# Moving the gate-logit fills of a transformer layer behind a group of products with the values

## The reference

```
x = x + 0.5 * ffn(layernorm(x))
x = x + attention(layernorm(x))      # 16 heads of 16, causal, softmax, output projection
x = x + 0.5 * ffn(layernorm(x))
```

```
probs = softmax(x @ gate_w.T)                    # 8 experts: the gate logits
top2_w, top2_idx = top_k(probs, 2)
counts = bincount(top2_idx); keep = counts <= cap   # cap = 1.25 * 8192 / 8
out = sum over the two experts of  keep * weight * expert(x)
```

## Time and profile before

| what | value |
|---|---|
| median of 3 runs | 1375.12 us |
| the profiled execution, its own time | 1374.71 us |
| its span | 1373.0 us |
| PE busy | 1273.9 us (93%) |
| DVE busy | 1093.9 us (80%) |
| ACT busy | 942.2 us (69%) |
| POOL busy | 397.3 us (29%) |
| chain that ended last | PE 61%, DVE 21%, ACT 6%, issue 3%, DVE's queue 3%, DMA 2% |

### The profile page before, as it was taken

How to read it: one execution, slowest core, us unless ns; L and a number is a source line. 1 busy time by engine, 2 the same in 40 slices (tenths; PEclk the granted TensorE clock), 3 DMA queues, 4 the chain that set the end, 5 groups by cost and what they waited for, 6 DMA issues and landing times.

```text
span 1373.0 us, 25088 instructions
## 1 busy us (share of the span) xinstructions
PE 1273.9 (93%) x8693; PEld 600.0 (44%) x8693; DVE 1093.9 (80%) x3527; ACT 942.2 (69%) x1697; POOL 397.3 (29%) x508
## 2 busy tenths in 40 slices
PE   6899999999999999999999999999999999999884
PEld 4433334444454444454444444544445544444332
DVE  6888888778887888878887788878888788779634
ACT  2257777777767777767767777677777677676752
POOL 3223322333232322332323332323222323222111
PEclk9889999999999999999999999999999999999977
DMA  4580443543325443324435423254442243340001
GB/s 134 114 156 13 70 70 58 100 75 74 68 37 100 90 70 70 61 63 89 70 59 101 83 62 68 40 101 89 70 70 53 38 92 70 58 69 32 1 1 34
DMA packets 57832, 95.18 MB, mean 69 GB/s; under 512 B 8352, under 2 KB 51488, under 8 KB 51744
## 3 DMA queue, kind: packets, MB, share of 16 engines
q1 hardware_dynamic: 55664, 92.30, 35.7%
q10 hardware_dynamic: 2032, 1.19, 0.3%
HBM read 59.91 MB, written 33.55 MB: 68 GB/s over the span
## 4 chain that ended last, share of the span: by engine, by line
PE 61%; DVE 21%; ACT 6%; issue 3%; DVEq 3%; DMA 2%; POOL 1%; SPq 1%; ACTq 0%; POOLq 0%
PE o_bank L1319 15%; PE s L1300 14%; PE st L1285 12%; DVE s L1011 8%; PE misc L1202 6%; PE misc L1186 4%; PE misc L1194 4%; DVE max_full L1015 3%; ACT probs L860 3%; PE misc L543 3%; DVE xn L519 2%; ACT q_stack L847 2%; DVEq L1022 2%; DVE stats L510 1%; DVE o_tok L1108 1%
## 5 line engine op out<-in xcount | busy, mean ns | idle before, releaser
L860 ACT ACTIVATE probs<-st 128x512 f32<-128x512 f32 (+1 forms) x1216 | 632.5, 581 | 192.2 <-PE st L1285 119.0
L1011 DVE CUSTOM_DVE_ANT_0 s<-s,causal 128x128 f32<-128x128 f32 (+3 forms) x1024 | 493.4, 502 | 131.9 <-PE s L1300 127.2
L1300 PE MATMUL s<-k_stack,q_stack 96*128 96x512 bf16 (+3 forms) x1536 | 493.7, 332 | 33.1 <-DVE max_full L1015 13.4
L1285 PE MATMUL st<-q_stack,k_stack 108*128 108x512 bf16 (+3 forms) x1536 | 486.8, 331 | 11.7 <-ACT probs L860 11.2
L1015 DVE TENSOR_REDUCE max_full<-s 128x1 f32<-128x512 f32 x512 | 349.7, 683 | 46.6 <-PE s L1300 46.3
L1319 PE MATMUL o_bank<-probs,v_aug 128*17 128x512 f32 (+3 forms) x3072 | 326.0, 496 | 5.4 <-POOL probs L734 5.2
L1300 PEld LDWEIGHTS s<-k_stack,q_stack 96*128 96x128 bf16 x1536 | 149.7, 98 | 373.1 <-DVE max_diag L1011 167.1
L734 POOL TENSOR_SCALAR_AFFINE_SELECT probs<-probs 128x512 f32<-128x512 f32 x256 | 163.5, 639 | 473.2 <-ACT probs L860 472.7
L1285 PEld LDWEIGHTS st<-q_stack,k_stack 108*128 108x128 bf16 x1536 | 149.8, 98 | 108.3 <-ACT probs L860 39.2
L746 POOL TENSOR_TENSOR qk<-qk,parts 128x512 f32<-128x512 f32 x64 | 75.0, 1171 | 282.4 <-ACT parts L820 282.4
L847 ACT ACTIVATE q_stack<-misc 12x2048 bf16<-12x2048 f32 x63 | 117.8, 1870 | 41.3 <-PE misc L1267 40.9
(11 more groups left out here) (115 smaller groups left out, 879.2 us busy)
## 6 DMA issues: line engine op xcount, KB each, us to landing
part_dram<-parts SPq DMA_DIRECT2D x128, 192.0 KB, 2.8
k_stack<-part_dram SPq DMA_DIRECT2D x186, 128.0 KB, 6.9
q_stack<-part_dram SPq DMA_DIRECT2D x31, 384.0 KB, 5.1
x_all<-x SPq DMA_DIRECT2D x16, 512.0 KB, 11.5
q_stack<-part_dram SPq DMA_DIRECT2D x31, 256.0 KB, 7.4
out<-x_all SPq DMA_DIRECT2D x7, 1024.0 KB, 10.6
q_stack<-part_dram SPq DMA_DIRECT2D x33, 128.0 KB, 9.0
k_stack<-part_dram SPq DMA_DIRECT2D x12, 64.0 KB, 3.0
```

Source lines behind the costliest of these rows:

```text
L860: nc.scalar.activation(probs[:, g % 2, h - part:h + 1, 0:width], st_bank[i % 3][:, 0:share * width] .rearrange("p (h c) -> p h c", c=width ...
L1011: nc.vector.tensor_tensor_reduce(out=bank, in0=bank, in1=causal[:, CW - width:CW], scale=1.0, scalar=-BIG, op0=ALU.add, op1=ALU.max, accum ...
L1285: score = nc.tensor.matmul(st_bank[i % 3][:, part * width:(part + 1) * width], k_stack[0:KROWS + MROWS, hg, h, jb * P:(jb + 1) * P], q_sta ...
L1300: nc.tensor.matmul(s_bank[u % 3][:, 0:width], q_stack[0:KROWS, hm, h, ib * P:(ib + 1) * P], k_stack[0:KROWS, hm, h, j0:j0 + width], start= ...
```

## The change

Two things change in the plan. First, in units that are multiples of four (those with a `pv`), `lg` and `lg0` events go from `extra` to `mid`, and so stand directly behind `pv` and ahead of `s`. Second, the units in `PLACE` are set to such multiples: `lg` 33 to 32 in step 2 and 31 to 32 in step 3; `lg0` stays at 12 in step 2 and goes from 11 to 12 in step 3.

```diff
-    "gate0": (4, 19, 23, 33, 36),
+    "gate0": (4, 19, 23, 32, 36),
...
-    "gate1": (4, 17, 26, 31, 37),
+    "gate1": (4, 17, 26, 32, 37),
...
-    "before": ((12, 16), (11, 29)),
+    "before": ((12, 16), (12, 29)),
...
     mid = {}
     for u, events in list(extra.items()):
+        if u % HG == 0:
+            mid[u] = [e for e in events if e[:2] in (("use", "lg"), ("use", "lg0"))]
+            events = extra[u] = [e for e in events if e not in mid[u]]
         for e in events:
             if e[0] == "use" and e[1] in PIECES:
```

## The result

The changed kernel takes 1372.01 us (median of 20 runs, 1370.48 to 1374.51), the kernel before 1374.3 us beside it (20 runs, 1372.34 to 1377.46): 0.9984 times, with a 95% interval of 0.9978 to 0.999. The forecast was a fall of 2.35 us, to 1372.8 us from the median then shown (1375.12). The size of the fall was met; two of its terms, for places B and C, were not, and they nearly cancel.

The account below looks back on a forecast made before the run. The bound changes hands within a batch: VectorE at A and C, TensorE at D, both close at B. 1.38 + 0.30 + 0.57 + 0.10 = 2.35 us off, 1372.8 us from the median 1375.12; range 1370.8 to 1376.2 us.

Parts of the forecast that it names:

- B: `lg` of step 2: VectorE takes the bound from TensorE, gain 0.05 us x 6 = 0.30 us in batches 1 to 6.
- C: `lg0` of step 3, 499.9 to 518.4 us: VectorE busy all along, gain 0, bounded by 0 and 0.45 x 6.
- D: `lg` of step 3, 518.4 to 532.0 us: TensorE-bound, shared column-tile visit saves 0.23 us x 6 = 1.38 us.
- A: `lg0` of step 2, 464.8 to 481.2 us: fill still waits for `o_tok`, score 0.78 us later, VectorE loses nothing; gain 0.
- from `st` 34 on TensorE is 0.23 us earlier: Step at B: behind the shared visit TensorE runs 0.23 us earlier, until it meets VectorE's shifted operations at the maximum of 496.68.
- 496.07 + 0.43 + 0.1 = 496.60: Step at B: VectorE's preceding operation, delayed 0.43 us, lets the maximum of 496.68 start at 496.60, leaving at most 0.08 us.
- Batch 0: First batch, no normalising on VectorE: 0.34 us at A and 0.23 us at C, together 0.57 us, between 0 and 0.8.
- Batch 7: Last batch: 0 at B; at D `ont` starts at 1334.0 instead of 1334.07; gain 0.10 us, between -0.3 and 0.58.
- Rival 1: Fill and `pv` do not share the column-tile visit; D gives 0, B costs 0.6 us: 1375.7 us, chance 0.18.
- Rival 2: At B VectorE packs small operations closer, so TensorE's 0.23 us come through: 1.1 us more, 1371.7 us; chance 0.22.
- rival 3: Maxima starve behind the fill at A, with B's delay uncovered too: 1380.4 us, 1377.9 with half of A; chance 0.07.
- Rival 4: Time saved at D ends in a wait before the next batch's VectorE stretch: 1374.2 us; chance 0.07.

Follow-up runs that it names:

- pair with the earlier unit: Kernel before and changed kernel, each with step 3's normalisation begun at unit 3 instead of 4: 1370.19 us (0.9979) and 1368.53 us (0.9971).
- C alone: Against the kernel before, only `lg0` of step 3 moved directly behind `pv`, the other three fills as before: 1373.77 us, 1.0009.
- D alone: Against the kernel before, only `lg` of step 3 moved directly behind `pv`, the other three fills as before: 1371.18 us, 0.9991.
- A, C and D: Changed kernel with `lg` of step 2 put back in unit 33 behind `s`, the other three fills moved: 1371.54 us, 0.9988 of the kernel before.

## Why the prediction came out right, term by term

**D** (forecast 1.38 us): right in mechanism and size. The visit is shared, the spacing is 1.95 us, and the chain keeps it: 0.24 us in D's interval of each of six batches, 1.44 us. With the fill behind the score the interval is as before.

**A** (0): right. The fill starts where it did, the score is 0.79 us later (forecast 0.78), VectorE is without idle time, and the interval stays at 14.21 us.

**B** (a gain of 0.30): wrong in sign. It is a loss of 0.05 us a batch, 0.3 us in all. The step that failed is "from `st` 34 on TensorE is 0.23 us earlier". It is not: the later maximum frees its score bank later, and the score that takes this bank waits for it (496.04), so the 0.23 us are gone before the place where I let both engines meet. I had followed the delay down VectorE's queue, but not back over the banks to TensorE. "496.07 + 0.43 + 0.1 = 496.60" failed besides: `max_rest` came at 497.38 - 0.91 = 496.47, 0.40 us later as foreseen, but lasts 0.20 us longer beside the selection, and the next maximum begins 0.29 us behind its start instead of 0.1. No run separates the two, but the times do in part. The score of 497.35 would let the maximum begin at about 497.61, by the 0.26 us between the two before (496.42 to 496.68): 0.02 us later than it was. VectorE takes it at 497.67, without idle time behind the long `max_rest`. So the wait for the bank alone takes the whole gain away, and so would the longer `max_rest` alone; the last 0.06 us are those of `max_rest`. The ends that I gave, -0.07 to +0.23, held the result.

**C** (0): right for TensorE, wrong as a sum. "The pattern of batch 2 repeats to 0.03 us at nearly all places" passed over this one, and the step "what is late next is VectorE, busy all along" treated VectorE's busy time as fixed, and it was not: an instruction in it is 0.40 or 0.88 us long, by where GpSimd's selection falls. In the traced kernel before, four batches of six were long: 4 x -0.28 + 2 x 0.21 = -0.7 us. The pair with the earlier unit, where this is taken away, gives 0.02 us a batch in C's interval (14.33 and 14.31).

**Batch 0** (0.57): 0.40. A gave its 0.34 us (13.62 to 13.26 in its interval). C gave 0.05 instead of 0.23: the `pv` ahead of the fill waits 0.19 us for GpSimd (195.51, `<-POOL probs`), and joining saves little behind a wait.

**Batch 7** (0.10): at D the step is confirmed and small, and at B one was missed. At D, from the start of `x_all` to `ont` it was 1334.07 - 1331.44 = 2.63 us, and is 1332.12 - 1329.64 = 2.48 now; before, and then after:

```profile
1331.44 0.69 DVE L1119 TENSOR_TENSOR x_all<-misc,x_all 128x512 f32<-128x512 f32 x1 [8.02 <-PE misc L1186]
```

```profile
1329.64 0.69 DVE L1122 TENSOR_TENSOR x_all<-misc,x_all 128x512 f32<-128x512 f32 x1 [7.15 <-PE misc L1189]
...
1331.05 0.62 PE L537 MATMUL misc<-xg_t,w_gate 128*32 128x128 f32 x16
...
1331.80 0.27 ACT L835 ACTIVATE lg_t<-misc 128x128 f32<-128x128 f32 x1
1332.12 0.66 PE L546 MATMUL misc<-ident,o_tok 128*128 128x128 f32 x4 [0.45 <-ACT lg_t L835]
```

`ont` waits 0.45 us for the copy of the logits behind the exponential, as the forecast had it; 0.15 us are won. At B the forecast was 0, and the interval is 20.02 to 20.04 us in all six traces of kernels with B moved, 19.84 to 19.86 in the seven with B as before: a loss of 0.19 us.

The stretch between the last two copies, which holds D of batch 7, is shorter by 1.02 us in this trace, and D explains only the 0.15. Its length and the granted clock of TensorE in it, with the same 139 matmul records each time:

| kernel | length, us | clock |
|---|---|---|
| before | 27.99 | 0.77 |
| after, both traces | 26.97 | 0.83 and 0.85 |
| C alone | 27.14 | 0.85 |
| D alone | 28.23 | 0.88 |
| A, C and D | 27.78 | 0.77 |

The clock changes between 1.2 and 2.4 GHz within the stretch and differs from kernel to kernel, but it does not order the lengths: D alone has the highest clock and the longest stretch. Why the changed kernel is 1 us shorter here stays open.

Together: 1.44 (D) - 0.3 (B) + 0.7 (C, with the `xn` as it fell in that trace) + 0.4 (batch 0) + 0.15 - 0.19 (batch 7) = 2.2 us, where 2.35 was forecast. Without the luck of C it is 1.5 us. So the forecast was met because an error of 0.6 us in B, with 0.2 more of it in batch 7 and 0.17 in batch 0, and an unseen 0.7 us in C nearly cancel. That is luck. The measured 2.3 us do not prove this sum to a tenth either: their interval goes from 1.4 to 3.0 us, and the same kernel measured again gave 0.8 us. The two traced executions differ by 1374.71 - 1372.64 = 2.07 us: the batches of the table give 2.31, batch 7 another 0.95 and the end 0.13, and the start of the changed kernel was 1.32 us longer.

**The rivals.** Rival 1 (the visit is not shared) falls by the 0.87 and 0.55 us at D. Rival 2 (B pays in full) falls by `mtr`, which is later, and rival 3 (the maxima starve) by VectorE without idle time at A. Rival 4 (D is absorbed) falls by D alone. (In rival 3, half of A's 4.7 us gives 1378.0 us, not 1377.9; nothing rests on it.)

## What to carry to other kernels

When two short visits of TensorE to column tiles stand apart, put them side by side: here it was worth 0.20 to 0.24 us each time where TensorE set the time, and nothing where VectorE did; of four places one paid in the steady batches. At B the move to an earlier unit cost a little more than the sharing gave, and at A and C VectorE sets the end. When an engine is "busy all along", look also at whether its instructions have one length: here a group with two lengths in the same trace was a meeting with GpSimd, and moving something by a few tenths of a microsecond paid or cost more than the edit itself. Measure such an edit with the collision moved away in both kernels, as with the `xn` one unit earlier, where 0.18 to 0.21 us a batch could be read off. And take intervals around each place out of the trace: they told apart what whole-kernel ratios, uncertain by 0.1%, could not.

## What the runs showed of the hardware

**A `tensor_scalar` of VectorE that meets GpSimd ends 0.15 us behind GpSimd's instruction.** Five meetings, from the rows above: 515.76 + 0.90 = 516.66 against 515.32 + 1.19 = 516.51; 677.73 + 0.88 = 678.61 against 678.46; 516.72 + 0.90 = 517.62 against 517.46; 518.80 + 0.60 = 519.40 against 519.26; 515.09 + 0.64 = 515.73 against 515.58. The difference is 0.14 to 0.16 us each time, whatever the overlap. When VectorE wins (517.84), GpSimd's selection pays, 0.81 instead of 0.64 us. The Trainium skill (SBUF — State Buffer, "Who interferes with whom") says that the two engines share a pair of ports, which `tensor_scalar` and `cast` can take and which an instruction with two inputs in SBUF needs against GpSimd's reads, that whichever issues first keeps the pair for its whole instruction, and that the other blocks. The trace agrees for the last `xn` that one side alone pays. The starts that it records don't show who keeps the ports: `xn` starts 0.09 to 0.10 us ahead in both outcomes. By a block until GpSimd's end the `xn` of 0.40 us would have ended at 678.86, and it ended at 678.61, so part of its work lies under the block. The `max_rest` of place B, with two inputs from SBUF, shows it too: 0.37 us instead of 0.17, and its end at 497.75 is 0.02 us behind that of the selection; so does the `CAST` of batch 1 (374.37 + 0.55 = 374.92, 0.03 us behind 374.25 + 0.64 = 374.89).

**Weights are loaded under running matmuls of the same rows.** The fill's first loads start at 531.57, within the `pv` of 531.13 that uses the same 128 rows, and no 0.10 us stand open. The Trainium skill (TensorE: Matmul & The Clock Gate, "The mechanism" of Part 3), from which I had drawn the reservation that such loads overlap only where the row group differs, also says that a load can be pulled ahead when it goes to the background weight buffer; the trace does not agree with the first and leaves room for the second, though it does not show which buffer was used.
